# One block for the front and the expert stage, with the first expert loads issued inside the front

## The reference

```
xn = layernorm(x)
q, k, v = xn @ wq.T + bq, xn @ wk.T + bk, xn @ wv.T + bv        # 16 heads of 16
off = tanh(pw_w @ gelu(depthwise_conv3(q)) + pw_b) * 6          # 12 samples per head
positions = clip(token + anchor(-2..2) + off, 0, 4095)
sk, sv = k and v read at the fractional positions (linear between neighbours)
attn = softmax(q.sk/4 - rel_scale*|positions - token|)
s = (attn . sv) @ wo.T + bo
scores = xn @ Wr.T + br                         experts
two best experts by scores + biases_N, gates = softmax values of the two, renormalised
y = sum over the two of gate * ((silu(xn@Wa + ba) * (xn@Wb + bb)) @ Wl2 + bl2)   # hidden 512
out = x + s * silu(y)
```

## Time and profile before

| | us |
|---|---|
| three runs, median (lowest to highest) | 1496.08 (1493.31 to 1501.79) |
| span of the profiled execution, first to last instruction | 1494.3 |
| PE busy | 1361.6 (91%) |
| DVE busy | 1280.2 (86%) |
| ACT busy | 823.8 (55%) |
| POOL busy | 804.3 (54%) |

### The profile page before, as it was taken

The page is one execution under the profiler, slowest core; times in us unless marked ns, Lnnn a source line. Parts: engine busy times, 40 slices in busy tenths (PEclk is TensorE's granted clock), DMA queues, the critical chain, the costliest instruction groups (busy, mean ns, idle before and its releaser), DMA issues.

```text
span 1494.3 us, 35841 instructions
## 1 busy us (share of the span) xinstructions
PE 1361.6 (91%) x13687; PEld 1085.4 (73%) x13688; DVE 1280.2 (86%) x1504; ACT 823.8 (55%) x1889; POOL 804.3 (54%) x566
## 2 busy tenths in 40 slices
PE   5998899984799999999999998999999978797988
PEld 4864565653688888888888886887888856675766
DVE  7837655556699999999999999999999999999961
ACT  2547687864445555555555554554555436574655
POOL 1001477773587766767666877768686651311111
PEclk9999999985999999999999999999999988898999
DMA  7933366564957676768677666767777679999897
GB/s 231 352 130 101 115 203 208 166 222 158 287 122 224 170 232 161 222 161 235 183 204 214 168 179 160 214 159 201 196 190 221 133 178 232 250 218 246 217 246 148
DMA packets 203481, 293.52 MB, mean 196 GB/s; under 512 B 24833, under 2 KB 160261, under 8 KB 203123
## 3 DMA queue, kind: packets, MB, share of 16 engines
q0 software_dynamic: 65792, 146.59, 38.5%
q1 hardware_dynamic: 134915, 144.84, 33.6%
q10 hardware_dynamic: 2672, 0.83, 0.2%
HBM read 182.83 MB, written 117.74 MB: 201 GB/s over the span
## 4 chain that ended last, share of the span: by engine, by line
DVE 48%; DMA 8%; PE 8%; issue 6%; SPq 5%; POOL 0%; ACT 0%; POOLq 0%; DVEq 0%
DVE gslope L1647 11%; DVE parts L1643 11%; DVE parts L1603 8%; DMA band<-band_rows 7%; DVE expert_mem L1569 5%; PE pB L1480 3%; DVE parts L1615 3%; SPq L1121 2%; DVE parts L1619 2%; DVE parts L1622 1%; PE pA L1465 1%; PE pY L1490 1%; DVE gslope L1700 1%; SPq L1115 1%; DVE wgt L1708 1%
## 5 line engine op out<-in xcount | busy, mean ns | idle before, releaser
L1175 POOL DMA_INDIRECT moe_rows<-expert_mem,token_of x142 | 324.9, 2288 | 76.2 <-issue 47.9
L1446 PE MATMUL pA<-xsT,expert_mem 128*128 128x256 f32 x1136 | 264.5, 387 | 22.6 <-DMA expert_mem<-in_w_l 15.5
L1156 POOL DMA_INDIRECT expert_mem<-xn_rows,token_of x142 | 222.3, 1566 | 96.8 <-issue 74.2
L1452 PE MATMUL pY<-expert_mem 128*128 x1136 | 265.7, 387 | 0.0
L1446 PEld LDWEIGHTS pA<-xsT,expert_mem 128*128 128x128 f32 x1136 | 220.3, 195 | 55.9 <-issue 20.0
L1446 PE MATMUL pB<-xsT,expert_mem 128*128 128x256 f32 x1136 | 256.8, 379 | 0.0
L1452 PEld LDWEIGHTS pY<-expert_mem 128*128 128x128 f32 x1136 | 211.1, 191 | 42.3 <-issue 16.2
L1446 PEld LDWEIGHTS pB<-xsT,expert_mem 128*128 128x128 f32 x1136 | 215.8, 190 | 29.3
L1643 DVE SCALAR_TENSOR_TENSOR parts<-pos_pair,prob 128x768 f32<-128x768 f32 x256 | 228.0, 953 | 1.1
L1647 DVE TENSOR_REDUCE gslope<-parts 128x256 f32<-128x3072 f32 x64 | 214.7, 3354 | 2.2
L1297 ACT ACTIVATE expert_mem<-pA,b1sel 128x256 f32<-128x256 f32 x284 | 111.3, 474 | 135.3 <-issue 93.2
(11 more groups left out here) (197 smaller groups left out, 2036.3 us busy)
## 6 DMA issues: line engine op xcount, KB each, us to landing
expert_mem<-in_w_l POOLq DMA_DIRECT2D x71, 1024.0 KB, 7.0
band<-band_rows SPq DMA_DIRECT2D x256, 96.0 KB, 5.5
S_rows<-stage SPq DMA_DIRECT2D x64, 376.0 KB
band_rows<-wgt SPq DMA_DIRECT2D x12, 1536.0 KB, 7.1
pos_pair<-pos_rows SPq DMA_DIRECT2D x28, 384.0 KB, 7.7
xn_rows<-stage SPq DMA_DIRECT2D x16, 512.0 KB, 5.4
v_rows<-stage SPq DMA_DIRECT2D x16, 512.0 KB, 4.2
moe_rows<-zeros POOLq DMA_DIRECT2D x4, 2048.0 KB
```

Source lines behind the costliest of these rows:

```text
L1156: nc.gpsimd.indirect_dma_start(out=xs[:, u, s], out_offset=None, in_=dram["xn"], in_offset=bass.IndirectOffsetOnAxis(ap=keep["inv"][:, 2 * ...
L1175: nc.gpsimd.indirect_dma_start(out=dram["moe"], out_offset=bass.IndirectOffsetOnAxis(ap=keep["inv"][:, 2 * n + s:2 * n + s + 1], axis=0), ...
L1446: mm = nc.tensor.matmul(dst[:, c], w1[:, 1 - u, k, o * HID + c * P:o * HID + (c + 1) * P], xsT[:, k], start=(k == 0), stop=(k == KC - 1))
L1452: mm = nc.tensor.matmul(pY[:, s], hid[:, h, c, s * P:(s + 1) * P], w2[:, c, ds(e * D, D)], start=False, stop=(s == 1 and c == HC - 1))
```

## The change

Both functions now write into one block (`EARLY_FROM` is 8, `EARLY_W2` is 2; `front_stored` lists the positions' and scores' stores, the pads, the gates and the bias), so there is no barrier between them; each engine goes from its front's last instruction to its first of the expert stage, and named waits take the barrier's place. The memory of k (`kT`) and the front's `stage` become parts of the array that later holds the expert weights and rows, with both slots of the first weights and the second weights' loads 0 and 1 over k of the first sequence, which is done with after group 7, and the second weights' loads 2 and 3 over k of the second.

```diff
+EARLY_FROM = GROUPS_PER_SEQ
+EARLY_W2 = SEQ // (EXPERTS * D)
@@ front, SP, loop over groups n
+                if n >= EARLY_FROM and n < EARLY_FROM + EARLY_W2:
+                    sp.wait_ge(s_done, EARLY_FROM * GROUP)
+                    keep["load_w2"](sp, n - EARLY_FROM)
             store_pos(STEPS - 2)
+            sp.wait_ge(s_done, TILES)
+            for k in range(EARLY_W2, HC):
+                keep["load_w2"](sp, k)
             store_pos(STEPS - 1)
-            sp.wait_ge(pads_set, 16 * 9)
-            sp.wait_ge(bias_stored, 16)
             for u in range(2):
-                sp.wait_ge(xn_stored[u], 16 * (STEPS // 2))
                 sp.wait_ge(v_stored[u], 16 * (STEPS // 2))
-                sp.wait_ge(pos_stored[u], 16 * (STEPS // 2))
-            for u in range(SX_SLOTS):
-                sp.wait_ge(sx_stored[u], 16 * STEPS)
@@ front, POOL
+            def first_w1():
+                pool.wait_ge(experts_known, 1)
+                pool.wait_ge(s_done, EARLY_FROM * GROUP)
+                for n in range(2):
+                    e = pool.value_load(keep["tile_exp"][0:1, n:n + 1], ...)
+                    pool.dma_start(keep["w1"][:, 1 - n], io["w_l1"][ds(e, 1), :, :]...)
             for q in range(4):
                 scatter(...)
                 clear_moe(q)
+                if q == 2:
+                    first_w1()
...
             pool.wait_ge(gates_stored, 16 * 4)
+            pool.wait_ge(pads_set, 16 * 9)
+            for u in range(2):
+                pool.wait_ge(xn_stored[u], 16 * (STEPS // 2))
+            pool.wait_ge(tokens_known, 1)
+            for n in range(2):
+                for s in range(2):
+                    nc.gpsimd.indirect_dma_start(out=keep["xs"][:, n, s], ..., in_=dram["xn"], ...)
@@ front, DVE, after the loop over groups
+            dve.wait_ge(list_loaded, 16)
+            chain(V.tensor_copy(list_f[:], spare_i[:]))
+            V.tensor_scalar(keep["inv"][:], list_f[:], float(TOKENS), None, ALU.add).then_inc(tokens_known, 1)
             offset_bias(STEPS - 1, 0)
             positions(STEPS - 2)
             offset_bias(STEPS - 1, 1)
-            dve.wait_ge(list_loaded, 16)
-            chain(V.tensor_copy(list_f[:], spare_i[:]))
-            V.tensor_scalar(keep["inv"][:], list_f[:], float(TOKENS), None, ALU.add)
             positions(STEPS - 1)
@@ mix
+        def front_over(eng):
+            eng.wait_ge(keep["front_pos_ready"], STEPS)
+            for stored, count in keep["front_stored"]:
+                eng.wait_ge(stored, count)
@@ mix, SP
+            front_over(sp)
             sp.dma_start(b2[:], ...)
-            sp.wait_ge(w1_loaded[0], 16)
-            for k in range(HC):
-                sp.dma_start(w2[:, k]...)
+            reload_slope(1)
...
-            for it in range(1, 3):
-                reload_slope(it)
+            reload_slope(2)
@@ mix, POOL
-            for n in range(2):
-                load_xs(n, n)
-                load_w1(n, n)
+            front_over(pool)
             nc.gpsimd.memset(wgt[:], 0.0).then_inc(zeroed, 1)
@@ mix, ACT
-            prepare(0)
             evacuate_x(0)
             take_expert(0, 0)
+            prepare(0)
+            for stored in keep["front_sx_stored"]:
+                act.wait_ge(stored, 16 * STEPS)
@@ mix, PE and DVE
+            pe.wait_ge(keep["front_s_ready"], TILES)
             transpose_x(0, 0, 0)
...
+            dve.wait_ge(keep["front_pads_set"], 16 * 9)
             V.memset(gslope[:, :, 0], 0.0)
```

More of the change, by code:

```diff
@@ L106 @@
 BAND_SKEW = BAND - 1
+W2_F, W1_F, HID_F = HC * EXPERTS * D, 2 * KC * 2 * HID, 4 * HC * PAIR
+ACT_F, XS_F, YS_F = 2 * HC * PAIR, 2 * 2 * XROW, 2 * 2 * D
+KT_PITCH = 8224
+W1_AT = KT_PITCH
+HID_AT = W1_AT + W1_F
+STAGE_AT = XS_AT = 2 * KT_PITCH
+ACT_AT = XS_AT + XS_F
+YS_AT = ACT_AT + ACT_F
+SHARED_F = YS_AT + YS_F
+EARLY_FROM = GROUPS_PER_SEQ
+EARLY_W2 = SEQ // (EXPERTS * D)
 PLACES = ("half products", "products", "half scores", "scores", "weights 0", "weights 1", "weights 2", "weights 3", "end")
@@ L156, in sem @@
         def sem(name):
-            return ctx.enter_context(nc.semaphore(name))
+            return keep["sems"].enter_context(nc.semaphore(name))
         qT, kT, scores = keep["qT"], keep["kT"], keep["scores"]
@@ L163, in front_block @@
         GROUP_F = GROUP * D
-        stage = sb("stage", [P, 4 * GROUP_F])
+        stage = keep["shared"][:, STAGE_AT:STAGE_AT + 4 * GROUP_F]
         xn = stage[:, 0:2 * GROUP_F].rearrange("p (u a c) -> p u a c", u=2, a=GROUP)
@@ L289, in front_block @@
         list_rows = sem("list_rows")
+        experts_known = sem("experts_known")
+        tokens_known = sem("tokens_known")
+        keep["front_pos_ready"], keep["front_s_ready"] = pos_ready, s_ready
+        keep["front_sx_stored"], keep["front_pads_set"] = sx_stored, pads_set
+        keep["front_stored"] = [(pos_stored[u], 16 * (STEPS // 2)) for u in range(2)] + [(sx_stored[u], 16 * STEPS) for u in range(SX_SLOTS)]
+        keep["front_stored"] += [(pads_set, 16 * 9), (gates_stored, 16 * 4), (bias_stored, 16)]
         scattered = sem("scattered")
@@ L313, in rows_of @@
             return slice(n * GTOK, (n + 1) * GTOK)
-        block = ctx.enter_context(nc.Block())
+        block = keep["block"]
         @block.sync
@@ L451, in _ @@
             pool.wait_ge(gates_stored, 16 * 4)
+            pool.wait_ge(pads_set, 16 * 9)
[4 more added lines that the diff above has]
+                for s in range(2):
+                    nc.gpsimd.indirect_dma_start(
+                        out=keep["xs"][:, n, s], out_offset=None, in_=dram["xn"],
+                        in_offset=bass.IndirectOffsetOnAxis(ap=keep["inv"][:, 2 * n + s:2 * n + s + 1], axis=0)).then_inc(
+                            keep["xs_loaded"][n], 16)
         @block.scalar
@@ L1002, in mix_block @@
         pJ = [pY[:, 0], pO[:, 0]]
-        w1_loaded = [sem(f"w1_loaded{u}") for u in range(2)]
-        w2_loaded = sem("w2_loaded")
+        w1_loaded, w2_loaded, xs_loaded = keep["w1_loaded"], keep["w2_loaded"], keep["xs_loaded"]
         wo_loaded = sem("wo_loaded")
@@ L1009, in mix_block @@
         b_loaded = sem("b_loaded")
-        xs_loaded = [sem(f"xs_loaded{u}") for u in range(2)]
         xsT_done = sem("xsT_done")
@@ L1773, in build, with load_w2 @@
         keep["slopes_in"] = slopes_in
+        shared = keep["shared"] = sb("expert_mem", [P, SHARED_F])
+        keep["w2"] = shared[:, 0:W2_F].rearrange("p (k n) -> p k n", k=HC)
+        keep["w1"] = shared[:, W1_AT:W1_AT + W1_F].rearrange("p (u k n) -> p u k n", u=2, k=KC)
+        keep["xs"] = shared[:, XS_AT:XS_AT + XS_F].rearrange("p (u s c) -> p u s c", u=2, s=2)
+        assert TOKENS + 1 + 2 * REACH <= KT_PITCH and W1_F <= SEQ + 1 and XS_F <= 4 * GTOK * D // P - SX_SLOTS * (SUBS // 2) * S_ROW
+        for name in ("xs_loaded", "w1_loaded"):
+            keep[name] = [ctx.enter_context(nc.semaphore(f"{name}{u}")) for u in range(2)]
+        keep["w2_loaded"] = ctx.enter_context(nc.semaphore("w2_loaded"))
+        keep["sems"] = ctx
+        def load_w2(eng, k):
+            eng.dma_start(keep["w2"][:, k].rearrange("p (e n) -> p e n", e=EXPERTS),
+                          io["w_l2"].rearrange("e (k p) n -> k p e n", p=P)[k]).then_inc(keep["w2_loaded"], 16)
+        keep["load_w2"] = load_w2
+        keep["block"] = ctx.enter_context(nc.Block())
         with nc.sbuf_tensor("scores", [P, TILES, EXPERTS], F32) as scores, \
-                nc.sbuf_tensor("qT", [P, KC, BATCH * (SEQ + 2)], F32) as qT, \
-                nc.sbuf_tensor("kT", [P, KC, TOKENS + 1 + 2 * REACH], F32) as kT:
+                nc.sbuf_tensor("qT", [P, KC, BATCH * (SEQ + 2)], F32) as qT:
+            kT = shared[:, 0:KC * KT_PITCH].rearrange("p (c n) -> p c n", c=KC)
             keep.update(scores=scores, qT=qT, kT=kT)
```

35 lines of the change are left out of this document (15 added, 20 removed).

## The result

The changed kernel takes 1486.12 us in the median (1480.93 to 1492.46, 6 runs) and the kernel before, timed beside it, 1497.26 us (1492.97 to 1504.54, 6 runs). The ratio is 0.9926, with a 95% interval of 0.9900 to 0.9951: 11.1 us faster. The same kernel was timed twice more beside the kernel before on other occasions: 0.9961 (0.9938 to 0.9984) and 0.9935 (0.9913 to 0.9957). The mean of the three is 0.9941, which is 9 us.

The account below looks back on a forecast made before the run. DVE was taken to bound the expert stage, its start of step 1's products (405.64) setting the end. Gains of 2.5 + 8.7 + 2.6 = 13.8 us gave a span of 1480.5 and a median of 1482.3 us, range 1475.5 to 1491.5.

Parts of the forecast that it names:

- 8.7 for slopes and positions: DVE's waits of 4.84 and 3.86 us for step 1's slopes and positions go; bounds 5 and 8.7 us.
- 2.6 for the gates: DVE's waits of 1.00 and 1.62 us at the gates of pairs 0 and 1 go; bounds 0 and 2.6 us.
- shift as a whole: Tail of 290.3 us: starts earlier by all of the 13.8 us gained, its length unchanged; bounds 0 to 13.8.
- the barrier's term: Between front and expert stage: without the barrier DVE starts its first products 2.5 us earlier; bounds 0 to 3.5.
- So 0 us: Early W1 and W2 loads inside the front cost nothing, since ACT never waited for a store slot.
- bound of 14.4 us: Upper bound for the early loads' cost in the front: 4 MB at 292 GB/s, all returning as ACT's slot waits.
- the slower rival: Early loads stretch the front through ACT's waits for store slots; 10.6 us lost, 1507 us, chance 0.06.
- the list's cover: Before the last offset_bias: the token list lands at 348.9, 1.5 us before DVE asks for it.
- list late: Late token_of delays the gathers, DVE starts at 364.75, 11.3 us gained, 1484.8 us; chance 0.15.
- PE's 17.8 us: PE's possible gain at the expert stage's start: pair 0 12.5 us earlier, plus ACT's 5.3 us at pair 3.
- The cover I had put at 6 us at gate 2: Expert stage: pair 2 ready by 396, DVE asking for its gate at about 402, so 6 us of cover.
- the change doesn't do what it says: Rival: gathers no earlier because token_of is late, DVE starts at 364.75, 11.3 us gained, 1484.8 us; chance 0.15.

Follow-up runs that it names:

- e5: Changed kernel with DVE's first twelve products of step 0 computed twice (10.5 us more work); ratio 1.0005 to the kernel before.
- e8: Kernel of e4 with the last positions' store put ahead of the last two W2 loads on SP's queue; 1484.96 us, ratio 0.9921.
- e10: The kernel of e8 timed and profiled again on another occasion, unchanged; 1480.92 us, ratio 0.9894.
- e2: Changed kernel with no early loads: W2 behind the last positions' store, W1 behind the first gathers; 1489.82 us, ratio 0.9961.
- e6: Changed kernel with only W1 loaded early, all four W2 loads behind the store of positions 14; 1483.43 us, one run.
- e1: Kernel before, barrier kept, with step 1's slopes and positions ahead of the W2 loads on SP's queue; 1495.24 us, ratio 0.9992.
- e7: Changed kernel with only two W2 loads early, the W1 loads behind the first gathers; 1484.68 us, one run.
- e3: Changed kernel once more, unedited, for a second profile; 1488.86 us, ratio 0.9961.
- e9: Changed kernel a third time, unedited, beside e10 on one chip; 1486.24 us, ratio 0.9935.
- e11: Kernel before with only the clears of moe_rows moved from POOL's queue to SP's, groups 0 to 7; 1499.29 us, ratio 1.0017.
- e4: Changed kernel with POOL's four 2 MB clears issued by SP as eight 1 MB pieces in groups 0 to 7; 1486.49 us, ratio 0.9929.

## Why the prediction held, and where its sum did not

**Right: what bounds, and what was removed.** DVE's start of step 1's products set the end, as read from the earlier trace rows. From DVE's first products to those of step 1 it took 40.89 us before, and 29.63, 29.63 and 29.64 in three profiles of after. The difference is 11.26 us; the two terms, 8.7 for slopes and positions and 2.6 for the gates, sum to 11.3. Behind it nothing moved: from step 1 to the last gate 798.64 us before and 798.34, 798.46 and 798.50 after.

**Right: it carries to the last gate. Not all of it: the tail.** e5 shows the first with its added 10.5 us. The three profiles of after say where the span's 9.0 us are (1485.1, 1487.2 and 1483.7, in the mean 1485.3, against 1494.3). Step 1 is at 395.38 in the mean (10.26 us earlier), the stretch to the last gate 0.2 us shorter and the tail 1.5 us longer (291.53 against 290.0). The tail was forecast to shift as a whole. Its length runs from 287.8 to 295.8 us over the thirteen profiles, and not quite at random: the seven profiles with both early loads have 290.7 to 295.8, the six others 287.8 to 290.6. Within one kernel, e8 reaches its last gate 6.8 us ahead of e10 and its end only 3.5. What makes the tail longer was not tested; it may be as little as chance in thirteen single executions.

**Wrong in size: the barrier's term, 2.5 us.** Its own mechanism was even underrated: 8.29 us from the last tanh to DVE's first products became 4.56, so 3.7 us went, a little over the best case of 3.5. (That takes rows that come early as well: in e2 it is 5.80 us, and in e6, with one block too but the rows behind W2, 8.80.) Counted from the last tanh, DVE's step 1 came 15.0 us earlier in the mean of the three profiles, more than the 13.8 us of the sum. But the term was to be read on DVE's start, and that moved from 364.75 to 365.06, 367.33 and 364.85: 1.0 us later in the mean. The step that failed is the one behind it, "So 0 us" for the early loads inside the front. The last tanh came 4.0, 6.3 and 3.8 us later, 4.7 in the mean. Of these 2.5 us lie between the tanhs of groups 7 and 15, and 2.2 in the groups before them, where the early loads had hardly begun (the first W2 is issued at 252.41 in after) and where executions differ anyway. The bound of 14.4 us held this, and the forecast took the lower end.

What lengthens the groups behind tanh 7 can be read off the thirteen profiles, up to tanh 14, ahead of the list:

```
clears of moe_rows           early loads   us from tanh 7 to tanh 14
POOL, four of 2 MB           none          102.26 (before), 103.28 (e1), 100.75 (e2)
POOL, four of 2 MB           W1 only        99.95 (e6)
POOL, four of 2 MB           W2 only       104.29 (e7)
POOL, four of 2 MB           both          103.81 (after), 105.75 (e3), 104.38 (e9), 105.79 (e5)
SP, 1 MB, groups 0 to 7      none          100.65 (e11)
SP, 1 MB, groups 0 to 7      both          100.08 (e4), 100.10 (e8), 100.34 (e10)
```

Beside POOL's clears both loads go with 2.8 us more (104.9 against 102.1 in the mean). Where no clear is left in this stretch, the same loads go with nothing (100.2 against 100.65). So the price is not one of the loads by themselves, but of loads and clears in one stretch, and "So 0 us" holds in the kernel of e4. These are single executions: the first and fourth line lie 0.5 us apart at their nearest, and which of the two loads it takes (e6, e7) is not settled. In e3 and e5 most of the excess lies in a single group (17.9 us between tanhs 10 and 11, where before has 15.5; 17.5 us between 7 and 8, where before has 14.4).

**Right on the absence of the slower rival's mechanism, wrong to conclude from it.** ACT still waited only for PE ahead of its score copies in after (total, times, longest; window 100 to 365):

```profile
ACT expert_mem L552 <- PE pS L676: 27.3, 27, 6.4
```

No store slot was ever late. I had asked only what waits for the stores. What the transfers meet besides is PE itself. Inside a tile's 64 equal matmuls, where nothing is waited for, PE pauses at a few places of the program that recur from kernel to kernel, and its trace calls it issue. Instructions are themselves fetched by transfers (the page above lists two instruction queues), and at such a place PE's seem to come late. Two of these places can be followed. One, near 306, in the profile of before and of e3, with the products right behind it:

```profile
306.64 0.31 PE L638 MATMUL pS<-kT,qm 32*64 32x47 f32 x3 [1.22 <-issue]
306.88 1.57 PE L650 MATMUL pOff<-pw_w,conv 128*128 128x192 f32 x8
```
```profile
299.40:318.60 19.20, 17.31 (x292) 11.09 (x291) 9.98 (x20) 12.53 (x24) 14.94 (x17) 0.91 1.00 322
...
311.22 0.41 PE L677 MATMUL pS<-expert_mem,qm 32*64 32x47 f32 x3 [1.89 <-issue]
...
311.55 2.93 PE L689 MATMUL pOff<-pw_w,conv 128*128 128x192 f32 x8
```

The pause lasts 1.22 us in before (DMA share 0.80 in 296 to 313), 1.30 in e9 (0.91), 1.95 in after (0.84) and 1.89 in e3, where the share is 1.00. In e3 the granted clock is 0.91 over this stretch, and the eight `pOff` matmuls right behind the pause take 2.93 us in place of 1.57: PE went on at the lower of its two levels. Between the two tanhs around it e3 takes 2.4 us more than before. e5 has the same at another place: a pause of 2.08 us up to 266.94, then the eight in 2.82 us. The lower level does not follow each such pause: behind the 1.95 us of after, and behind 2.33 us in e7 (up to 265.79), the eight take 1.57 us.

The other place, near 345, has 0.79 us in before, 3.77 in after and 3.79 in e9, and it looked like the whole explanation. It isn't: e2 has 3.77 there with no early load, e7 0.77 with two, and e3 and e5, which have the two longest stretches, 1.41 and 1.05. Read over the thirteen profiles, and not tested by itself, it goes with when the last 2 MB clear was issued. In after, e9 and e2 the pause begins 7.3 us after that (336.13 and 343.45 in after), with the clear still on its way (9.1 us to land in after); in before, e1, e3, e5 and e7, where PE gets there 10.6 to 13 us after it, the pause is 0.77 to 1.41 us; e6 has 2.08 us, 4.8 us after it. In the four kernels whose clears are all issued by group 7 it is 0.79, 0.61, 0.62 and 0.41.

From tanh 7 to 14 PE's pauses of this kind add up to 4.2 to 7.1 us in the four profiles with both loads and POOL's clears, 2.3 to 4.9 in the three without the loads, and 0.8 to 2.2 in the four without POOL's clears. That fits the table above, and was not tested alone: the granted clock goes the same way (0.87 to 0.90, 0.88 to 0.92, 0.91 to 0.93), and e3 and e5, which have the longest stretches with only 4.2 and 4.9 us of pauses, are the two in which the lower level came early. How much of the 2.8 us the pauses are, and how much the clock, stays open.

**Half wrong: the list's cover.** It was to be read at 344.9, land at 348.9 and lie 1.5 us ahead of DVE. It was read at 350.05 and landed 4.3 us later, while the front was later as well, and DVE took it at 354.58 right behind an addition of 0.56 us from 354.11. No wait arose, but the cover was about nought. The case "list late" was a fair one: e6 paid for it, with the 5.14 us of wait shown above.

**Wrong, without a price here: PE's 17.8 us.** PE's pair 0 began at 363.85 (forecast 360.5) and its pair 2 at 390.88, only 3.9 us earlier than in the earlier trace rows, pair 3 7.6 us earlier. I took 366 for the release of POOL, with 373 at worst, and it was 373.9: the last positions' store stood on SP's queue from 363.69 behind 2 MB of W2, and landed 10 us later. Behind it the gather of pair 2 took 4.98 us beside DVE's addition of 5.76 us (378.46 and 376.86 above), as the rule of the Trainium skill, page "SBUF — State Buffer", section "SBUF: two separate sides", had it (the page names for it a DVE instruction with two SBUF inputs beside a GpSimd one that reads SBUF). In e8 it ran beside DVE's products, about 0.9 us each, and took 3.79 us, more than the wait for one such product gives. The cover I had put at 6 us at gate 2 was 3.8, and 0.6 at gate 6. The forecast that DVE stays the bound was thus right by less than 1 us. Had PE been a few us worse, part of the 11.3 us would have gone back into waits at the gates, as in e1.

**Range and chances.** The measured 1486.12 us lies inside 1475.5 to 1491.5. It is also the most favourable of the three timings (11.1, 5.8 and 9.7 us by their ratios). It lies nearest to the rival "the change doesn't do what it says" (1484.8, with DVE's start unmoved and 11.3 us left), to which I gave 0.15, but for another reason than the list. The forecast came near by a sum of terms that was right within 1.2 us up to step 1 (15.0 for 13.8) and lacked two subtractions: 4.7 us in the front (about half of it before the early loads, so partly the luck of a short front in the one profile of before) and 1.5 us in the tail. The stretch of the front was weighed only as part of a slower outcome, not as a few us off the likeliest one, and there it belonged.

## What to carry to other kernels

When work is moved into a stage that is bound elsewhere, ask not only what waits for its buffers but what the added traffic does to the bounding engine itself; look for idle time put down to issue inside runs of equal instructions, and price a few us for it even where no wait names a transfer. A small store that releases other engines goes ahead of bulk loads on its queue: here that went with 3.6 to 5.5 us more lead of PE, which shows in no single time but is what the next saving on DVE will need. And take the steps apart before crediting the striking one: here the barrier's removal was worth 3.7 us with rows that came early, and nothing with rows that came late (e6); the front that came with it was as much longer; and the order on one queue gained nothing that the times could tell by itself (e1), and with one block most of the 11 (e2).

## What the hardware showed beyond that

The same matmul run is interrupted for 0.4 to 3.8 us at one place of the program, by kernel and by execution, without any wait of its own, and at other places the lower clock followed such a pause in two executions (1.89 and 2.08 us of pause, then 2.93 and 2.82 us for what takes 1.57), and did not in two others (1.95 and 2.33 us). At the place near 345 it was 3.8 us in the three profiles in which a 2 MB transfer had been issued 7.3 us before (one of them shows it landing after 9.1 us), 2.1 us in one where that was 4.8 us before, and 0.4 to 1.4 us in the nine others. The same early loads cost 2.8 us beside the 2 MB clears and nothing where the clears had been issued before them. And an execution's first 250 us vary by 7 us and its last 290 us by 8 (over all thirteen profiles), while the 798 us between them repeat within 0.3 us over before and the three of after.
